# Layernorm transposes moved from TensorE to VectorE blocks and DMAs, in a pre-norm attention and spiking feed-forward layer

## The reference

```python
x = x + attn(layernorm(x))      # 8 heads of 128, softmax inside blocks of 64 tokens
x = x + ffn(layernorm(x))

# attn: q, k, v = x @ Wq + bq, x @ Wk + bk, x @ Wv + bv, in blocks of 64 tokens
#       probs = softmax(q k^T / sqrt(128)); out = (probs v) @ Wo + bo
# ffn:  h = square(relu(x @ W_fc^T))          # 1024 -> 4096
#       y = h @ W_proj^T                      # 4096 -> 1024
#       five steps of mem = 0.9 * mem + y - reset; the result is the mean of (mem > 1)
# layernorm(x) = (x - mean) / sqrt(var + 1e-5), over the 1024 features
```

## Time and profile before

| | us |
|---|---|
| median of three runs | 729.07 |
| the profiled execution | 728.92 |
| its span, slowest core (core 5) | 727.3 |
| TensorE busy | 715.1 (98%) |
| VectorE busy | 369.6 (51%) |
| ScalarE busy | 196.4 (27%) |
| Pool busy | 26.1 (4%) |

### The profile page before, as it was taken

The page is one execution under the profiler, slowest core; times in us unless marked ns, Lnnn a source line. Parts: engine busy times, 40 slices in busy tenths (PEclk is TensorE's granted clock), DMA queues, the critical chain, the costliest instruction groups (busy, mean ns, idle before and its releaser), DMA issues.

```text
span 727.3 us, 11110 instructions; the slowest of 8 cores (725.3 to 727.3 us)
## 1 busy us (share of the span) xinstructions
PE 715.1 (98%) x3988; PEld 337.6 (46%) x3988; DVE 369.6 (51%) x645; ACT 196.4 (27%) x354; POOL 26.1 (4%) x53
## 2 busy tenths in 40 slices
PE   7999999999999999999999999999999999999996
PEld 3544444454454444444444444444444444444444
DVE  5325655766575666524755224755224656321476
ACT  3543440561264044121102331201332111332000
POOL 2210000000001000000000000000000000000000
PEclk9999999999999999999999999999999999999999
DMA  8996863185249998697312001312101111100011
GB/s 181 211 152 152 146 132 129 59 209 117 111 100 234 178 213 205 161 190 171 117 58 104 12 1 59 114 61 78 38 0 55 62 59 58 59 1 1 30 43 45
DMA packets 19061, 74.66 MB, mean 103 GB/s; under 512 B 2240, under 2 KB 2496, under 8 KB 16576
## 3 DMA queue, kind: packets, MB, share of 16 engines
q0 software_dynamic: 6768, 31.46, 24.1%
q1 hardware_dynamic: 9792, 34.08, 14.4%
q10 hardware_dynamic: 2448, 8.40, 3.0%
HBM read 82.33 MB, written 16.78 MB: 136 GB/s over the span
## 4 chain that ended last, share of the span: by engine, by line
PE 93%; DMA 5%; DVE 1%; issue 1%; POOL 0%; DVEq 0%; POOLq 0%
PE ps_m L375 31%; PE ps_y L444 29%; PE ps_m L320 13%; PE ps_m L348 8%; PE ps_m L362 8%; DMA wq_sb<-Wq 4%; PE ps_t L302 2%; PE ps_y L397 1%; PE ps_y L425 1%; DVE acc_sb L682 1%; DMA xr<-x 1%; PE ps_t L409 0%; DVE acc_sb L679 0%; POOL wq_sb L768 0%; DVE xr L687 0%
## 5 line engine op out<-in xcount | busy, mean ns | idle before, releaser
L375 PE MATMUL ps_m<-xn2t,w_sb 128*128 128x512 bf16 x1024 | 224.6, 379 | 0.0
L444 PE MATMUL ps_y<-w_sb,h_sb 128*128 128x512 bf16 (+1 forms) x1024 | 220.2, 376 | 0.0
L375 PEld LDWEIGHTS ps_m<-xn2t,w_sb 128*128 128x128 bf16 x1024 | 98.8, 98 | 117.6
L444 PEld LDWEIGHTS ps_y<-w_sb,h_sb 128*128 128x128 bf16 x1024 | 99.7, 98 | 114.8 <-issue 0.3
L529 ACT ACTIVATE h_sb<-ps_m 128x512 bf16<-128x512 f32 x128 | 76.4, 597 | 241.1 <-PE ps_m L375 241.1
L672 DVE TENSOR_TENSOR h_sb<-h_sb 128x512 bf16<-128x512 bf16 x128 | 53.5, 424 | 122.1 <-ACT h_sb L529 122.1
L682 DVE SCALAR_TENSOR_TENSOR acc_sb<-ps_y,acc_sb 128x1024 bf16<-128x1024 f32 (+2 forms) x72 | 78.6, 1092 | 7.5
L320 PE MATMUL ps_m<-xnt,wk_sb 128*128 128x512 bf16 x248 | 58.7, 380 | 0.8 <-DMA wk_sb<-Wk 0.8
L348 PE MATMUL ps_m<-wv_sb,xnt 128*128 128x512 bf16 x256 | 58.6, 380 | 0.0
L320 PE MATMUL ps_m<-xnt,wq_sb 128*128 128x512 bf16 x240 | 56.9, 380 | 1.0 <-DMA wq_sb<-Wq 1.0
L679 DVE TENSOR_SCALAR acc_sb<-ps_y 128x1024 bf16<-128x1024 f32 (+2 forms) x18 | 19.6, 1091 | 73.7 <-PE ps_y L444 73.6
(11 more groups left out here) (61 smaller groups left out, 378.3 us busy)
## 6 DMA issues: line engine op xcount, KB each, us to landing
xr<-x SPq DMA_DIRECT2D x32, 512.0 KB, 6.5
xl<-x SPq DMA_DIRECT2D x24, 512.0 KB, 5.3
w_sb<-Wfc POOLq DMA_DIRECT2D x8, 1024.0 KB, 13.8
x<-xr ACTq DMA_DIRECT2D x16, 512.0 KB, 3.5
w_sb<-Wpr POOLq DMA_DIRECT2D x8, 1024.0 KB, 31.1
out<-xr POOLq DMA_DIRECT2D x12, 512.0 KB, 2.9
wq_sb<-Wq POOLq DMA_DIRECT2D x8, 256.0 KB, 8.1
wk_sb<-Wk POOLq DMA_DIRECT2D x8, 256.0 KB, 8.1
```

Of the source, the lines that this page charges most:

```text
L375: m = E.matmul(bank(key)[:], w1_sb[fc // 4][:, k0:k0 + 128], xn2t[t % 2][:, c * 512:(c + 1) * 512], start=(c == 0), stop=(c == 7))
L444: return E.matmul(out, h_sb[fc][:, tt * 128:(tt + 1) * 128], w2_sb[fc // 4][:, k0:k0 + n], start=(fc == 0), stop=(fc == 31))
```

## The change

Units 0 to 7 stay as they are. For the 24 others there is no `turn_x` and no `turn_copy`: right behind `ln_scale` VectorE transposes the 128x1024 unit in blocks of 32x32 (`ln_blocks`) into a tile `blk`, and when the four units of a tile are there, SP issues 16 DMAs (`turn_tile`) that bring each 32 rows of the blocks to their partitions in the tile that TensorE reads. For that the rows of a unit are loaded in another order: a unit now has 32 tokens of each 128 of the tile. There is one tile `xn2t` instead of two, so the DMAs of the tiles 5 to 7 wait for the last `up` group of the part before. The three `blk` tiles lie where space is free at their time. A load of x2 waits for all four stores of its part.

```diff
 def ln_turn(b, s):
-    return ln_unit(b, s, 3 if b == -1 else 4)
+    return ln_unit(b, s, 3) if b == -1 else None
+
+BY_DMA = 8
...
+    def blocks_of(n):
+        return blk[0 if n < 4 else 1 if n == 4 else 2]
+
+    def tile_turned(n):
+        if n < 2:
+            return turned_copied(4 * n + 3)
+        return ld_turn[n % 2], 256 * (n // 2)
...
             if h == 0 and kind == "q":
-                E.wait_ge(*turned_copied(4 * p + 3))
+                E.wait_ge(*tile_turned(p))
...
             if fc == 0:
-                E.wait_ge(*turned_copied(16 + 4 * t + 3))
+                E.wait_ge(*tile_turned(4 + t))
...
-                    if t < 3 and tt in (1, 2) and fc % 16 == 0:
-                        turn_x(16 + 4 * (t + 1) + 2 * (tt - 1) + fc // 16)
...
+            if i >= BY_DMA:
+                ln_blocks(i)
+
+        def ln_blocks(i):
+            n, u = divmod(i, 4)
+            if u == 0 and n in (3, 6, 7):
+                E.wait_ge(*tile_turned(n - 1))
+            E.wait_ge(ve_xn, i + 1)
+            dst = blocks_of(n)[:].rearrange("p (j u t) -> p j u t", j=32, u=4)
+            E.transpose(dst[:, :, u, :],
+                        xn[i % 2][:].rearrange("p (j t) -> p j t", j=32)).then_inc(ve_blk, 1)
...
         def xl_load(i):
-            src = rows(x_h, i) if i < 16 else rows(x2_h, i - 16)
+            n, u = divmod(i, 4)
             if i >= 10:
                 E.wait_ge(ve_xn, i - 1)
-            if i >= 16:
-                E.wait_ge(st_x2[i % 4], 16 * ((i - 16) // 4 + 1))
-            E.dma_start(out=xl[i % 2][:], in_=src).then_inc(ld_xl[i % 2], 16)
+            if n >= 4:
+                for tt in range(4):
+                    E.wait_ge(st_x2[tt], 16 * (n - 3))
+            src = (x_h if n < 4 else x2_h)[n % 4 * 512:(n % 4 + 1) * 512, :]
+            E.dma_start(out=xl[i % 2][:],
+                        in_=src.rearrange("(i u t) d -> u i t d", i=4, u=4)[u]).then_inc(ld_xl[i % 2], 16)
...
+        def turn_tile(n):
+            E.wait_ge(ve_blk, 4 * n + 4 - BY_DMA)
+            if n < 4:
+                E.wait_ge(*filled(("v", n - 2, 3, 1)))
+            elif n > 4:
+                E.wait_ge(*filled(("up", n - 5, 31)))
+            src = blocks_of(n)[:].rearrange("p (c a k) -> p c a k", c=8, a=4)
+            dst = ln_tile(n)[:].rearrange("p (c i k) -> p c i k", c=8, i=4)
+            for i in range(4):
+                for a in range(4):
+                    E.dma_start(out=dst[32 * a:32 * a + 32, :, i, :],
+                                in_=src[32 * i:32 * i + 32, :, a, :]).then_inc(ld_turn[n % 2], 16)
...
             for i in (4 * b + 12, 4 * b + 13):
                 xl_load(i)
+            turn_tile(b + 2)
         for tt in range(4):
             xr_load(3, tt)
...
                 for i in (4 * t + 22, 4 * t + 23):
                     xl_load(i)
+                turn_tile(5 + t)
```

More of the change, by code:

```diff
@@ L138, in turn_order @@
                 keys.append(("pt", b, h))
-    keys += [("x", i) for i in range(20, 32)]
     return {k: n for n, k in enumerate(keys)}
@@ L182, in build_nc @@
     h_sb = [at(f"h_sb_{i}", WORK + 1024 * i, 512, BF16) for i in range(32)]
-    xn2t = [at("xn2t_0", WORK + 49152, 4096, BF16), at("xn2t_1", WORK + 57344, 4096, BF16)]
+    xn2t = at("xn2t", WORK + 49152, 4096, BF16)
+    blk = [at("blk_0", W1A + 32768, 4096, BF16), at("blk_1", WORK, 4096, BF16),
+           at("blk_2", WORK + 57344, 4096, BF16)]
     w1_at = [W1A + 8192 * i for i in range(6)] + [WQ, WQ + 8192]
@@ L238, in build_nc @@
     full_x, free_x = sem("full_x"), sem("free_x")
+    ve_blk = sem("ve_blk")
+    ld_turn = [sem(f"ld_turn{i}") for i in range(2)]
     full_s, free_s = sem("full_s"), sem("free_s")
@@ L283, in turn_bank, with ln_tile @@
         return ps_x[i] if 1 <= i <= 3 else ps_t[:]
-    def ln_target(i):
-        return xnt[i // 4 % 2] if i < 16 else xn2t[i // 4 % 2]
+    def ln_tile(n):
+        return xnt[n % 2] if n < 4 else xn2t
+    def blocks_of(n):
[4 more added lines that the diff above has]
+        return ld_turn[n % 2], 256 * (n // 2)
     def tensor_program(E):
@@ L375, in up_group @@
                 m = E.matmul(bank(key)[:], w1_sb[fc // 4][:, k0:k0 + 128],
-                             xn2t[t % 2][:, c * 512:(c + 1) * 512],
+                             xn2t[:, c * 512:(c + 1) * 512],
                              start=(c == 0), stop=(c == 7))
@@ L510, in turn_copy @@
             E.wait_ge(*turned(i))
-            dst = ln_target(i)[:].rearrange("p (c t) -> p c t", c=8)
+            dst = ln_tile(i // 4)[:].rearrange("p (c t) -> p c t", c=8)
             E.copy(dst[:, :, (i % 4) * 128:(i % 4 + 1) * 128],
@@ L586, in scalar_program @@
                 i = 20 + 4 * t
[L587 to L594, removed]
+                for j in range(4):
+                    ln_rstd(i + j)
     def vector_program(E):
@@ L617, in ln_scale @@
             E.wait_ge(ac_rstd, i + 1)
-            if i >= 2:
+            if 2 <= i < BY_DMA + 2:
                 E.wait_ge(*turned(i - 2))
+            elif i >= BY_DMA + 2:
+                E.wait_ge(ve_blk, i - 2 - BY_DMA + 1)
             E.tensor_scalar(xn[i % 2][:], src[:], mv[i % 2][:, 0:1], rstd[i % 2][:, 0:1],
                             ALU.subtract, ALU.mult).then_inc(ve_xn, 1)
+            if i >= BY_DMA:
[8 more added lines that the diff above has]
+                        xn[i % 2][:].rearrange("p (j t) -> p j t", j=32)).then_inc(ve_blk, 1)
         def softmax_shift(p, h):
```

## The result

The changed kernel takes 780.75 us (779.5 at the lowest, four runs), where before has 729.3 in the same comparison: a ratio of 1.069 (95% interval 1.067 to 1.072), slower by 51 us. The forecast was slower, 757 us, its own case from 749 to 768 and the widened range from 744 to 780. The side and the main cause were right, the size was short by 24 us: 28 us of loss were forecast and 51 came, less than 1 us past the upper end of the widened range. (One of the four executions was disturbed and is left out of the ratio.)

A forecast was written before the change was run, and what follows sets the result against it. The prediction took TensorE, busy 98% of the span, to bound the kernel. 728.9 - 10.8 (turns) + 36 (wait for tile 4) + 2.5 (clock) = 756.6, forecast 757 us; own range 749 to 768, widened 744 to 780.

The forecast's parts named there:

- What bounds the kernel, and what leaves TensorE: TensorE bounds the kernel, busy 98% of the span; 24 turns of 0.45 us leave it, worth 10.8 us.
- VectorE's part: One block transpose per unit on VectorE, 1.2 us each, 29 us in all, hidden in its idle time: no cost.
- The packets of a tile: Each tile's 16 DMAs of 64 KB make 256 packets of 256 bytes per DMA, 256 packets per engine.
- A packet alone: A 256-byte packet with nothing beside it takes 25 ns, bounds 17 and 54.
- One packet per queue and turn: A busy DMA engine gives every queue one packet in turn, whatever its size, so a tile is charged 256 turns.
- Tile 4: Units 16 to 19: the tile queues beside weight loads, lands at 289.5, and TensorE waits 36 us (34 to 42).
- Rivals B and C: B: a DMA's 16 pieces share one turn, 725 us, chance 0.07; C: small packets pass large ones, 718.1 us, 0.10.
- Tiles 2, 3 and 5 to 7: These tiles land before TensorE wants them, all hidden; tiles 2 and 3 have 5 us of slack.
- Rival D: DMAs of 256 packets issue slowly, 1.6 us each; tiles 2 and 3 cost 11 us each, 781 us; chance 0.06.
- The clock: After TensorE's long pause its clock may start low, costing 2.5 us (0 to 5).
- What the queues get: Step costing the 96 tile DMAs on SP's queue, packet by packet, alone and beside other loads.
- two steps of slack: Softmax steps behind a block transpose in VectorE's queue have slack over 3 us, so its 1.2 us is hidden.

The follow-up runs named there:

- e3: The kernel after with each xl load cut into four DMAs and weight loads from w1(5) on waiting for tile 4: 723.8 us, 0.991 of before.
- e4: The kernel before with only the permuted xl loads taken from after, turns still on TensorE: 746.6 us, 1.023 of before.
- e1: The kernel after with each xl load cut into four DMAs of 32 rows: 756.8 us, 1.035 of before.
- e10: The kernel after with xl loads in four DMAs and Pool waiting for tile 4 between w1(5) and w1(6): 720.0 us, 0.987 of before.
- e7: e5 with 8 of the 16 DMAs of tile 4 issued on ACT's queue instead of SP's: 731.1 us, 1.002 of before.
- e5: e1 with the tile laid out so that its DMAs move rows of 2 KB instead of 256-byte pieces: 752.3 us, 1.031 of before.

## Why the prediction was right, and where it was short

- **What bounds the kernel, and what leaves TensorE:** right. The best versions gain 9.5 to 9.7 us of the 10.8.
- **VectorE's part:** right. 1.245 us against 1.2, 29.9 us in all, hidden, as e3 shows.
- **The packets of a tile:** right. Of the 28064 packets under 512 bytes in after, 1952 are those of e4; the other 26112 are 272 for each of the 96 DMAs, which is 256 pieces and 16 semaphores.
- **A packet alone:** 25 ns forecast. From 300 to 304 us in after 1713 packets, semaphores among them, fill 53.5% of 16 engines: 20 ns.
- **One packet per queue and turn**: right. In e1, from 240 to 250 us, with 256-byte pieces and semaphores on q1:

```profile
q0 software_dynamic: 199, 1.38, 83.4%
...
q1 hardware_dynamic: 201, 0.05, 3.6%
```

  The bias packets of the earlier trace rows are some 18 times shorter than those beside them (11 and 203 ns by share and count), not ten, which speaks for the rule all the more.

- **Tile 4:** forecast 36 us, 34 to 42; 37.2 in after and 35.7 in e1. Rivals B and C are refuted by these. The number is better than its parts, and in after its agreement is in part luck: the blocks were done at 242.9 us and TensorE asked at 270.8, where 228.3 and 253.5 were forecast, both late by the same loads. Left out were the semaphore packets, which take turns too, and the pace of the end: SP's queue stood still for 38 us at its third DMA and needed 0.64 us for each of the last ones, so the tail was limited by issuing and not by packets:

```profile
248.62 37.99 SPq L886
...
305.02 0.59 SPq L886
```

- **Tiles 2, 3 and 5 to 7:** forecast hidden, with 5 us to spare for tile 2. They are, but for 1.5 us on tile 2, whose 16 issues took 17.5 us with SP held up four times, for 1.4 to 2.6 us. It landed at 128.2, not near 121. With the xl loads cut in four there is no such wait (e1, e3). (The blocks of tile 5 are done at 357.1 by the earlier trace rows, not 358.4; nothing hangs on it.)
- **Rival D:** its number, 781, is the measured one by coincidence. It wanted 1.6 us per issue and 11 us of wait on each of tiles 2 and 3; an issue that nothing held took 0.59 us, and the waits were 1.5 us and none.
- **The clock:** forecast 2.5 us for one pause. It was 1.8 behind tile 4 in after and 3.0 in e1, and in after 5.0 behind two pauses that were not foreseen.
- **The step that failed** is "What the queues get". It counts the DMAs of `turn_tile` and passes over the changed `xl_load`, which the diff shows: same bytes, same 4 KB rows, the same one DMA, but a source of 4 x 32 rows. That put each load on 4 engines. Missing from the sum: 15.1 us of softmax waits and 5.0 of clock behind them; e1 against after gives 24 us for both, with the 1.5 each on tiles 2 and 4. With this term the sum 756.6 would have been 777. It also undid the "two steps of slack" under "What VectorE gets": that slack covers a step of 1.2 us, not a load of 20 that VectorE waits for in the middle of its queue.

## What to carry to other kernels

When the pattern of a load changes, count the engines that it will run on: the semaphore packets of a DMA, and the share of 16 engines while it runs alone, tell them. A transfer that must land at a given time is costed in turns, packets and semaphores together, beside each backlogged queue (one that always has a packet ready), and not in bytes. Here it paid more to hold back what was backlogged (720 us, e10) or to use a second queue (731, e7) than to make the packets larger (752, e5). A rearrangement that is free for its own engine can still be lost to a load that stands in the middle of an in-order engine's queue.

## What the hardware showed that was not expected

- The 4-byte semaphore packet of a DMA takes a full turn of a backlogged engine, 0.88 us on the mean beside two other queues (e5, 250 to 274 us).
- A DMA of 64 KB with 256 packets takes SP 0.59 us to issue even when nothing holds it, and one of 32 packets of 2 KB takes 0.59 us as well, so here the issue did not depend on the number of packets.
- A queue whose packets don't get their turn stops its issuing sequencer: SP stood 38 us at one DMA, and what comes later in its program, here the xr loads, could not start.
